# Second expert rows of token group 2: scaled by ScalarE and added by GpSimd instead of VectorE

## What is computed

```python
vals = take_along_axis(scores, idx, axis=1)          # two gates per token, k = 0 and 1
for each expert e:                                    # hidden width 128
    h = silu(xt @ w1[e] + b1[e]) * (xt @ w2[e] + b2[e])
    y += gate[:, e] * (h @ w3[e] + b3[e])
z = silu(xt @ sw1 + sb1) * (xt @ sw2 + sb2) @ sw3 + sb3   # shared expert, hidden width 256
return x + y + z
```

## Time and profile before

| | |
|---|---|
| median of 3 runs | 261.38 us (259.18 to 262.07) |
| profiled execution, whole time | 260.76 us |
| profiled execution, span of the trace | 258.9 us |
| PE busy (matmuls) | 241.5 us, 93% of the span |
| VectorE (DVE) busy | 149.7 us, 58% |
| GpSimd (POOL) busy | 111.8 us, 43% |
| ScalarE (ACT) busy | 78.7 us, 30% |
| mean granted TensorE clock | 0.993 of 2.4 GHz |

### The profile page before, as it was taken

The page is one execution under the profiler, slowest core; times in us unless marked ns, Lnnn a source line. Parts: engine busy times, 40 slices in busy tenths (PEclk is TensorE's granted clock), DMA queues, the critical chain, the costliest instruction groups (busy, mean ns, idle before and its releaser), DMA issues.

```text
span 258.9 us, 4022 instructions
## 1 busy us (share of the span) xinstructions
PE 241.5 (93%) x1092; PEld 162.9 (63%) x1093; DVE 149.7 (58%) x314; ACT 78.7 (30%) x169; POOL 111.8 (43%) x135
## 2 busy tenths in 40 slices
PE   7847988999999889999999999999999999999695
PEld 6715756788875346667777777777777744444241
DVE  0599899649979977434333333333444401498982
ACT  2223535413147100333343333333333321111300
POOL 7782455410020344456666666666665321000720
PEclk9999999999999999999999999999999999999979
DMA  6998686697326938954555444455444224999853
GB/s 199 341 416 326 249 302 240 248 321 294 142 101 253 425 114 242 363 175 156 173 171 163 130 150 156 133 166 167 169 168 139 84 86 171 396 387 387 322 191 134
DMA packets 20699, 57.91 MB, mean 224 GB/s; under 512 B 2533, under 2 KB 2533, under 8 KB 20428
## 3 DMA queue, kind: packets, MB, share of 16 engines
q1 hardware_dynamic: 15084, 39.89, 42.2%
q0 software_dynamic: 5600, 17.83, 20.8%
HBM read 40.94 MB, written 17.30 MB: 225 GB/s over the span
## 4 chain that ended last, share of the span: by engine, by line
PE 81%; DVE 13%; DMA 3%; issue 2%; ACT 0%; DVEq 0%
PE psum L578 72%; PE psum L724 6%; DVE r L977 4%; DVE xT L1207 3%; DVE xT L972 2%; DVE xT L946 2%; DVE xT L987 2%; PE psum L621 2%; PE psum L737 2%; DMA late_region<-xt_rows,from_row 1%; DMA xT<-cond_pack 1%; DVE mix_bias L974 0%; ACT late_region L842 0%; DVE r L1163 0%; DVEq L1166 0%
## 5 line engine op out<-in xcount | busy, mean ns | idle before, releaser
L578 PE MATMUL psum<-wexp,r 128*128 x272 | 68.5, 381 | 0.3 <-DVE r L1163 0.2
L578 PEld LDWEIGHTS psum<-wexp,r 128*128 128x128 f32 x272 | 48.4, 190 | 22.8 <-issue 16.9
L946 DVE TENSOR_TENSOR r<-psum,ebias 128x256 f32<-128x256 f32 x34 | 14.4, 424 | 64.2 <-PE psum L578 64.2
L490 POOL DMA_INDIRECT late_region<-xt_rows,from_row x36 | 35.6, 990 | 23.9 <-issue 16.6
L496 POOL DMA_INDIRECT expert_rows<-late_region,to_row x33 | 33.3, 1010 | 26.8 <-issue 18.3
L578 PE MATMUL psum<-wexp,xt_sb 128*128 x68 | 34.8, 594 | 0.0
L883 ACT ACTIVATE r<-r 128x128 f32<-128x128 f32 x34 | 10.5, 310 | 57.6 <-DVE r L946 57.6
L578 PE MATMUL psum<-xT,shared_sb 128*128 128x512 f32 x64 | 28.0, 594 | 0.0
L889 ACT ACTIVATE late_region<-psum 128x512 f32<-128x512 f32 x34 | 20.3, 598 | 13.9 <-PE psum L578 13.9
L1163 DVE COPY r<-psum 128x512 f32<-128x512 f32 x36 | 24.5, 679 | 0.0
L724 PE MATMUL psum<-ident,late_region 128*128 128x128 f32 x144 | 21.6, 273 | 1.0 <-DMA late_region<-xt_rows,from_row 1.0
(11 more groups left out here) (175 smaller groups left out, 311.0 us busy)
## 6 DMA issues: line engine op xcount, KB each, us to landing
wexp<-expert_pack SPq DMA_DIRECT2D x16, 768.0 KB, 5.3
wexp<-expert_rows SPq DMA_DIRECT2D x8, 1024.0 KB, 12.8
xt_rows<-xt_sb SPq DMA_DIRECT2D x16, 256.0 KB, 2.8
x_early<-x SPq DMA_DIRECT2D x2, 1024.0 KB, 8.1
late_region<-x SPq DMA_DIRECT2D x2, 1024.0 KB, 12.7
ebias<-expert_bias SPq DMA_DIRECT2D x1, 2048.0 KB, 7.1
out_dram<-x_early SPq DMA_DIRECT2D x8, 256.0 KB, 9.7
shared_sb<-shared_pack SPq DMA_DIRECT2D x1, 1536.0 KB, 16.4
```

What stands on the lines that cost most here:

```text
L490: nc.gpsimd.indirect_dma_start(out=xg[:, slot, :], out_offset=None, in_=xt_dram[:, :], in_offset=bass.IndirectOffsetOnAxis(ap=index.bitcas ...
L578: return nc.tensor.matmul(dst, lhsT, rhs, start=start, stop=stop)
L946: return nc.vector.tensor_tensor(dst, a, b, op)
```

## The change

For group 2 the second expert rows (k = 1) are handled as those of group 3 were. ScalarE scales eight tiles (8 to 15) in place of four and waits for each group's rows first. GpSimd adds eight in place of four. VectorE adds the rows with k = 0 alone in groups 2 and 3, and waits for each tile's GpSimd addition before it does. The semaphores are renamed, since they now count both groups.

```diff
@@ gpsimd, at its end
             pool.wait_ge(x_again_loaded, 16 * (NT - EARLY * GT))
-            for u in range(GT):
-                t = LAST * GT + u
-                pool.wait_ge(last_scaled, u + 1)
-                nc.gpsimd.tensor_tensor(acc_tile(t), acc_tile(t), rows_k[:, LAST, 1, u, :], op=ALU.add
-                                        ).then_inc(last_added, 1)
+            for t in range(EARLY * GT, NT):
+                pool.wait_ge(late_scaled, t - EARLY * GT + 1)
+                nc.gpsimd.tensor_tensor(acc_tile(t), acc_tile(t), rows_k[:, t // GT, 1, t % GT, :], op=ALU.add
+                                        ).then_inc(late_added, 1)
@@ scalar, at its end
-            act.wait_ge(rows_loaded[LAST], 16 * TOPK)
-            for u in range(GT):
-                rows = rows_k[:, LAST, 1, u, :]
-                t = LAST * GT + u
-                nc.scalar.activation(rows, rows, ACT.Copy, scale=tops[:, 1, t:t + 1]).then_inc(last_scaled, 1)
+            for t in range(EARLY * GT, NT):
+                if t % GT == 0:
+                    act.wait_ge(rows_loaded[t // GT], 16 * TOPK)
+                rows = rows_k[:, t // GT, 1, t % GT, :]
+                nc.scalar.activation(rows, rows, ACT.Copy, scale=tops[:, 1, t:t + 1]).then_inc(late_scaled, 1)
@@ vector, add_rows(g)
-                ks = range(TOPK) if g < LAST else [0]
+                ks = range(TOPK) if g < EARLY else [0]
                 for k in ks:
                     for t in range(g * GT, (g + 1) * GT):
-                        if g == LAST:
-                            dve.wait_ge(last_added, t % GT + 1)
+                        if g >= EARLY:
+                            dve.wait_ge(late_added, t - EARLY * GT + 1)
```

More of the change, by code:

```diff
@@ L270, in adaln_moe_ffn @@
         rows_loaded = [sem(f"rows_loaded{g}") for g in range(NG)]
-        last_scaled = sem("last_scaled")
-        last_added = sem("last_added")
+        late_scaled = sem("late_scaled")
+        late_added = sem("late_added")
         out_ready = sem("out_ready")
```

## The result

The median of 20 runs is 261.59 us, against 260.96 for 20 runs of the kernel before; the ratio is 1.0057, with a 95% interval from 1.0033 to 1.0081. The ratio leaves disturbed runs out and stands for 1.5 us (interval 0.9 to 2.1); the two medians differ by 0.63.

A forecast was written before the change was run, and what follows sets the result against it. PE was taken to bound the kernel, with its wait for VectorE's group 2 additions on the chain. Four fewer additions, a later start and more turns gave +0.74 us: 261.5 profiled, 262.1 from the 261.38 median; range 259.6 to 263.9.

The forecast's parts named there:

- The bound: Before tile 12, PE waits for VectorE's shared addition of tile 8; the wait was to grow from 2.08 to 2.83 us.
- The handoffs: Delays from ScalarE to GpSimd and from GpSimd to VectorE at the start of group 2's additions, each taken as 0.16 us.
- The first rival: VectorE's tile 8 gets in before GpSimd's tile 9, so turns end 0.27 us earlier than before: 261.1 us, chance 0.14.
- The scalings: ScalarE's four added scalings of group 2, after the last silu, from 236.96 to 239.5, were to cost nothing.
- The turns: In group 2 VectorE ends 0.55 us after GpSimd, GpSimd 1.13 after VectorE; VectorE's last row addition ends at 245.90.
- The low clock: TensorE's clock at 0.50 after PE's wait, slowing tiles 12 and 13, was to cost the same 1.54 us.
- The slower rival: After PE's longer wait the low clock lasts twice its 3.4 us, over tiles 14 and 15: 263.7 to 264.4, chance 0.12.
- Group 3: The last group's GpSimd additions and VectorE's row and shared additions were to have room, the shared ones following PE.
- The cover: Slack before VectorE's last shared addition, which could begin at 253.8, would itself delay the end: 2.6 us.
- the prediction's signs: Expected in the new profile: L1207 at 1.7 us, PE's wait 2.8 us, the last four L946 each ended by PE.
- the sum: VectorE's last row addition of group 2 and the end come 0.74 us later: 261.5 us profiled, median 262.1.

The follow-up runs named there:

- e1: The changed kernel, but GpSimd begins group 3 only when VectorE's row additions of group 2 are done; median 259.25 us, PE's wait 1.69 us.
- e2: The kernel before, but GpSimd begins group 3 only when VectorE's row additions of group 2 are done; median 258.19 us, ratio 0.9934.
- e4: The changed kernel with one extra GpSimd addition on unused data ahead of tile 8's; median 264.16 us, PE's wait 3.67 us.
- e3: The changed kernel with ten extra products of the unit matrix on PE in its wait before tile 12; median 260.28 us.
- e10: The kernel before with seven extra products of the unit matrix on PE in its wait before tile 12; median 260.30 us.
- e5: The changed kernel with group 2's order turned round: VectorE adds k = 0 rows first, GpSimd follows, shared additions wait for GpSimd; median 260.07 us.
- e8: The kernel before without ScalarE's scalings and GpSimd's additions, VectorE adding all rows; median 258.76 us, ratio 0.9956.
- e9: The kernel before with GpSimd's additions of group 3 put off about 0.5 us by a short addition on unused data; median 259.53 us.

## Why the prediction was right

**The bound.** PE's wait for tile 8's shared addition was the one place where the change could act, and it is there that it acted: 2.08 to 2.70 us (forecast 2.83).

**The handoffs.** ScalarE to GpSimd was taken at 0.16 and is 0.16; GpSimd to VectorE, which the trace before did not show, was bounded by 0 and 0.16 and is 239.19 - 239.05 = 0.14 (GpSimd's tile 8 ran 237.78 to 239.05). The first rival, VectorE getting in before tile 9, could not have won with any handoff: GpSimd's tile 9 started at 239.02, before tile 8 had ended. The rows before had shown the same (242.90 against 242.94), so its chance of 0.14 was too high.

**The scalings.** They were free, as forecast: group 2's rows were there, and no wait for them shows. They began at 236.92, 0.59 us after the silu's start (236.33), before the silu's own 0.69 were over. The forecast let the one follow the other without overlap, 0.72 after the silu's start (236.96 against 236.24), 0.13 too late, which is as much as 2.83 and 2.70 differ by.

**The turns.** Forecast 0.55 and 1.13, measured 0.54 to 0.56 and 1.12 to 1.13. The last row addition was forecast at 245.90 and ended at 245.86. e1 and e2 show that these turns, and not the amount of work, lengthen PE's wait: each one that is taken away takes 1.0 us off it. e4 shows that VectorE's later start counts in full beside them. Of the rule that the first to start holds the ports for its whole instruction (the Trainium skill, SBUF — State Buffer, section "SBUF: two separate sides"), the blocking is confirmed in all seven steps, but a turn of both takes 1.68 us (240.76 to 242.44), not the 2.00 that two whole instructions would take.

**The low clock.** Forecast the same 1.54 us; tiles 12 and 13 took 5.35 us, less 3.88, 1.47. The slower rival, a longer low clock, did not occur in the trace, and not in e4 with a wait of 3.67 us either. That it hangs on PE's idle time is shown by e3 and e10. The runs agree: 7 of 11 in e1 and 5 of 10 in e3 have a mean clock of 0.998 or more, and none of 20 of the changed kernel.

**Group 3.** GpSimd was to end at 249.5 and ended at 249.45; the last shared additions were due at 254.54 and 256.48 and came at 254.45 and 256.39, each waiting for PE. The cover held. Of the prediction's signs one was not met: it had the last four shared additions each ended by PE, and only the last two were. Its own working, with VectorE's row additions lasting until 252.0, left no such wait for tile 12.

**The size.** That the profiled execution rose by exactly the forecast 0.74 us is partly luck. The tail grew by 0.55 (12.49 to 13.04): 0.62 of wait more, 0.07 of low clock less. The rest was in no term of the sum: PE ended group 2 0.10 later (244.04 for 243.94), and 0.1 lies outside the span. The forecast median of 262.1 was 0.5 too high, since it stood on the first three runs' 261.38, where 20 runs gave 260.96.

Against the measured ratio of 1.0057, which is 1.5 us, +0.74 lies just under the interval (0.9 to 2.1). The prediction took the profiled execution for the kernel before; that kernel also has runs of 258 us (10 of the 79 beside the experiments show a clock of 1.000), and the changed kernel has none above a clock of 0.993 in 20. If those are runs with a turn less, as is argued under e10, the changed kernel can't have them: GpSimd is at work on group 2 before VectorE starts, so a later landing of group 3 spares no turn. Runs at a mean clock of 0.993 alone differ by what was forecast, 261.44 less 260.69 is +0.75, but the two sets were not run side by side.

## What to carry to other kernels

Before work is moved from VectorE to GpSimd, look in the trace at what a VectorE instruction with two SBUF operands takes while GpSimd adds: here 1.75 us for 0.74, so that an addition moved away saved 0.66 us and each one left behind paid 1.0. Where a moved step has to precede what is left (the same accumulator), put the engine that others wait for first and let the helper follow, as e5 did with the same work: PE's wait went, though the time at the median was the kernel before's (ratio 1.0006). And before sharing, price the version that doesn't: VectorE alone (e8), and GpSimd held back until the urgent rows were done (e2), both came out under the kernel before (by 0.4 and 0.7%, the first only just clear of none) and, not run side by side, under the changed one.

## What was not expected of the hardware

Holding an engine back made the tail shorter. With a short extra addition ahead of GpSimd's own (e9) VectorE's rows took 0.76 us less and the tail 2.46 us less, since the turn behind the short addition cost 0.26 us, not 1.0, and no low clock followed. Held back altogether (e2), GpSimd took no turn there, and VectorE's rows took 2.02 us less.

A wait of PE of 1.32 us (e9) or 1.69 us (e1) left the granted clock at 1.00, and waits of 2.08, 2.70 and 3.67 us were followed by a stretch at 0.50 that cost about 1.5 us. Each is one trace, and the length of a wait alone does not decide it: early in the kernel before, PE waited 2.17 us for VectorE, and the granted clock was 1.00 over the whole stretch.

```profile
19.29 1.12 PE L578 MATMUL psum<-x_early,r 128*128 128x512 f32 x2 [2.17 <-DVE r L977]
...
12.00:54.00 42.00, 34.32 (x207) 24.46 (x206) 35.65 (x74) 17.45 (x28) 21.61 (x20) 1.00 0.82 300
```

So the first microsecond taken off such a wait can be worth more than one: e1 took 1.01 us off the wait and 2.5 us off the tail.
